# A gated cross-attention and expert network on one core: other queue and row orders in the first and last stage, and in the third two of four heads of P turned by VectorE and transfers

## The reference

```python
x = x + tanh(g_xattn[0]) * L0_xattn(layernorm(x), ctx)   # 16 heads, latent keys with rope, no mask
x = x + tanh(g_ffn[0])   * L0_ffn(layernorm(x))          # top 2 of 8 experts, low-rank terms, gelu
x = x + tanh(g_xattn[1]) * L1_xattn(layernorm(x), ctx)   # 16 heads of 32, causal softmax
x = x + tanh(g_ffn[1])   * L1_ffn(layernorm(x))          # relu, softmax over 8, V then U

# L1_xattn
qp = q @ Wq.T;  k, v = split(latent_kv @ Wkv_expand.T)
scores = einsum('bhqd,bhkd->bhqk', qh, kh) / sqrt(32);  scores = where(causal, scores, min)
out = einsum('bhqk,bhkd->bhqd', softmax(scores), vh) @ Wout.T
```

## Time and profile before

| | us |
|---|---|
| median of 3 runs | 1366.28 (1364.13 to 1367.78) |
| the profiled execution's own time | 1366.01 |
| its span | 1364.2 |
| DVE busy | 937.1 |
| ACT busy | 519.0 |
| POOL busy | 408.3 |
| first stage, about | 0 to 415 |
| second stage, about | 415 to 1010 |
| third stage, about | 1010 to 1212 |
| fourth stage, about | 1212 to 1364 |

### The profile page before, as it was taken

How to read it: one execution, slowest core, us unless ns; L and a number is a source line. 1 busy time by engine, 2 the same in 40 slices (tenths; PEclk the granted TensorE clock), 3 DMA queues, 4 the chain that set the end, 5 groups by cost and what they waited for, 6 DMA issues and landing times.

```text
span 1364.2 us, 20490 instructions
## 1 busy us (share of the span) xinstructions
PE 1338.5 (98%) x7532; PEld 1083.8 (79%) x7532; DVE 937.1 (69%) x1803; ACT 519.0 (38%) x1569; POOL 408.3 (30%) x463
## 2 busy tenths in 40 slices
PE   7999999999999999999999999999999999999999
PEld 5788888888878788778887888788876788878777
DVE  5666676675775878785778667866888777746533
ACT  2545445455554321231123111311137777712220
POOL 3113313232255343101111111114418865530000
PEclk9999999999999999999999999999999999999999
DMA  8655444443563232210221012112333131144431
GB/s 273 211 164 172 153 157 149 151 157 125 179 208 97 80 94 71 81 39 16 67 89 43 20 43 90 31 58 66 116 110 121 46 103 63 56 142 147 136 124 54
DMA packets 120136, 146.73 MB, mean 108 GB/s; under 512 B 14157, under 2 KB 75725, under 8 KB 120037
## 3 DMA queue, kind: packets, MB, share of 16 engines
q1 hardware_dynamic: 120036, 145.44, 33.5%
HBM read 101.35 MB, written 44.04 MB: 107 GB/s over the span
## 4 chain that ended last, share of the span: by engine, by line
PE 84%; DVE 9%; DMA 2%; SPq 1%; issue 1%; POOL 1%; ACT 1%; DVEq 0%; ACTq 0%; POOLq 0%
PE bank L118 80%; PE bank L121 3%; SPq L170 1%; DVE AH L130 1%; DVE STG L130 1%; DVE st L152 1%; DVE XR L140 1%; DVE PYZ L164 1%; DMA XR<-scr 1%; DVE sm L143 1%; DMA PYZ<-pscr 1%; DVE PT L130 0%; DVE XR L137 0%; DVE AH L127 0%; ACT STG L124 0%
## 5 line engine op out<-in xcount | busy, mean ns | idle before, releaser
L118 PE MATMUL bank<-XT,AR 128*128 128x512 f32 x1152 | 280.2, 393 | 0.1
L118 PE MATMUL bank<-AR 128*128 128x512 f32 x1056 | 260.5, 396 | 1.1 <-DVE PTV L127 0.7
L118 PEld LDWEIGHTS bank<-XT,AR 128*128 128x128 f32 x1152 | 213.9, 188 | 48.5 <-issue 1.5
L124 ACT ACTIVATE STG<-bank,b1c 128x512 f32<-128x512 f32 x128 | 88.3, 690 | 387.2 <-PE bank L118 319.2
L118 PEld LDWEIGHTS bank<-AR 128*128 128x128 f32 x1056 | 193.7, 188 | 46.1 <-DVE AR L130 1.5
L118 PE MATMUL bank<-AR,CT 128*128 128x512 f32 x768 | 191.3, 392 | 0.0
L118 PE MATMUL bank<-AR,AH 128*128 128x512 f32 x768 | 185.8, 390 | 0.0
L127 DVE CAST AH<-STG 128x512 fp32r<-128x512 f32 x192 | 91.3, 475 | 112.8 <-PE bank L118 98.8
L118 PEld LDWEIGHTS bank<-AR,AH 128*128 128x128 f32 x768 | 143.6, 188 | 30.7 <-issue 1.1
L118 PEld LDWEIGHTS bank<-AR,CT 128*128 128x128 f32 x768 | 140.1, 188 | 27.0 <-issue 0.4
L127 POOL CAST BA<-STG 128x256 fp32r<-128x256 f32 x64 | 31.2, 488 | 395.9 <-PE bank L118 251.8
(11 more groups left out here) (142 smaller groups left out, 1858.1 us busy)
## 6 DMA issues: line engine op xcount, KB each, us to landing
XR<-scr SPq DMA_DIRECT2D x64, 256.0 KB, 2.9
pscr<-PYZ SPq DMA_DIRECT2D x30, 512.0 KB, 2.7
PYZ<-pscr SPq DMA_DIRECT2D x120, 128.0 KB, 3.0
XR<-in_x_dram SPq DMA_DIRECT2D x32, 256.0 KB, 4.1
XR<-lscr SPq DMA_DIRECT2D x128, 64.0 KB, 2.0
scr<-XR SPq DMA_DIRECT2D x32, 256.0 KB, 2.1
STG<-in_WoT_dram SPq DMA_DIRECT2D x8, 512.0 KB, 5.3
STG<-in_Wq_dram SPq DMA_DIRECT2D x8, 512.0 KB, 5.9
```

The source lines that it names most:

```text
L118: return self.e.matmul(o, w, x, start=start, stop=stop, skip_group_check=True) if self.e else Nothing()
L124: return self.e.activation(o, x, func, **kw) if self.e else Nothing()
```

## The change

Third stage: heads 0 and 1 of P are no longer transposed by PE. DVE transposes their 32 x 32 blocks into `P3Y` (columns 2048 to 3071 of `STG`, which were slots 4 and 5 of the weights; four slots are left), SP stores them to `pscr` and loads them back in four transfers into the first half of `PTV`. AV reads them from there in four runs of 32. AV of u moves from the end of step u+2 to behind Q of step u+3. K stands ahead of the output blocks and transposes on PE, and ahead of the final additions on DVE. ACT does exponential 3 ahead of the copies of P, and all its mask seeds ahead of them. The norms of tiles (2,1,0) and (2,1,1) go from POOL to DVE. SP issues the store and the loads of P at the head of each step.

First stage: rows are loaded ahead of the first weights, two tiles are transposed ahead of `prep_a(0)`, DVE's norms stand ahead of its splits; a tile load and `prep_b(4)` go ahead of the loop on SP, later weight loads and `ln_store` go ahead of `p_store`; on DVE norm and block transpose go ahead of `pv1(u - 3, (1,))` and `blocks1`. Fourth stage: `ln_load(3, 2, .)` stands between V transfers of tile 0, `ln_load(3, 3, .)` ahead of those of tile 1.

```diff
+        P3Y, P3Z = STG[:, 2048:3072], PTV[:, 0:1024].rearrange("p (j n c) -> p n j c", j=4, n=8)
@@ tensor: opening
-            ln_turn(0, 0, 0, ring4.next())
+            for tb in range(2):
+                ln_turn(0, 0, tb, ring4.next())
             prep_a(0)
-            for tb in range(1, 4):
+            for tb in range(2, 4):
                 ln_turn(0, 0, tb, ring4.next())
@@ tensor: turn3, av3
-                for b in range(4):
+                for b in (2, 3):
                     k = ps.take(("pt3", u, b), ring.next())
...
+                pe.wait_ge(*d_p3[u, 3])
...
+                        o = k[32 * j:32 * j + 32, 128 * b:128 * b + 128]
+                        if j < 2:
+                            ins = pe.matmul(o.rearrange("p (a c) -> p a c", a=4), V3[:, b, 32 * h:32 * h + 32],
+                                            P3Z[:, 4 * j + b], True, True)
@@ tensor: step of the third stage
                     q3(u, ring3)
+                if u >= 3:
+                    av3(u - 3, ring3)
                 if u > 4 and g == 2:
                     v3(m)
+                if 0 < u < 16:
+                    k3(u, ring3)
+                if u == 1:
+                    v3(0)
                 for block in wo_at(u):
                     wo3(*block)
                 if u >= 2:
                     turn3(u - 2, ring3)
-                if 0 < u < 16:
-                    k3(u, ring3)
-                if u == 1:
-                    v3(0)
...
-                if u >= 2:
-                    av3(u - 2, ring3)
+            av3(15, ring3)
@@ scalar: step of the third stage
                     exp3(u - 1, (0, 1))
+                if u >= 3:
+                    av3(u - 3)
                 if values:
                     v3(m, 1)
                 if 1 <= u <= 16:
-                    exp3(u - 1, (2, 3) if project else (2,))
-                if seeded(u):
-                    for j in range(len(by_vector(u)), 3):
-                        seed3(u, j)
+                    exp3(u - 1, (2,))
                 if values:
                     v3(m, 3)
-                if values:
+                if 1 <= u <= 16:
                     exp3(u - 1, (3,))
+                if seeded(u):
+                    for j in range(len(by_vector(u)), 4):
+                        seed3(u, j)
                 if u >= 2:
                     turn3(u - 2, 2)
                     turn3(u - 2, 3)
@@ vector
-            ln_turn(0, 0, 0)
-            prep_a(0)
             ln_pre(0, 0, 3)
             ln_norm(0, 0, 2)
+            ln_turn(0, 0, 0)
             ln_norm(0, 0, 3)
-            for tb in range(1, 4):
-                ln_turn(0, 0, tb)
+            ln_turn(0, 0, 1)
+            prep_a(0)
+            ln_turn(0, 0, 2)
+            ln_turn(0, 0, 3)
...
+            def turn_p3(u):
+                for j in range(2):
+                    e.wait_ge(*nm3_ok[u, j])
+                    if u:
+                        e.wait_ge(*t_p3[u - 1])
+                    e.turn(blocks_out(P3Y)[:, 4 * j:4 * j + 4],
+                           blocks_in(P3[:, u % 2, 0:1024])[:, 4 * j:4 * j + 4]).then_inc(*p3y_ok.mark((u, j)))
...
                     q3_out(u)
+                if u >= 2:
+                    turn_p3(u - 2)
+                if u == 2:
+                    ln_norm(2, 1, 0)
+                    ln_norm(2, 1, 1)
...
-                if u >= 3:
-                    av3(u - 3)
                 if 1 <= u <= 16:
                     inverse(u - 1, 0)
                     inverse(u - 1, 1)
...
+                if u >= 3:
+                    av3(u - 3)
                 if u > 4 and g == 2:
                     v3(m)
+                if 1 < u < 16:
+                    k3(u)
                 for block in wo_at(u):
                     final3(*block)
-                if u >= 2:
-                    turn3(u - 2, 0)
-                    turn3(u - 2, 1)
@@ sync: opening and first stage
-            ln_load(0, 0, 1)
+            for tb in range(1, 4):
+                ln_load(0, 0, tb)
             prep_a(0)
-            ln_load(0, 0, 2)
-            ln_load(0, 0, 3)
...
             prep_a(4)
+            ln_load(*after1(0), 0)
+            prep_b(4)
...
+                if u == 2:
+                    prep_a(5)
+                    prep_b(5)
+                if u == 3:
+                    prep_a(6)
+                if u < NU and 3 <= p <= 6:
+                    ln_store(*after1(m), p - 3)
                 if 1 <= u < 31:
                     p_store(u - 1)
-                if u == 1:
-                    prep_b(4)
-                    prep_a(5)
-                if u == 2:
-                    prep_b(5)
-                    prep_a(6)
@@ sync: third stage
+            def p3_store(u):
+                e.wait_ge(*p3y_ok[u, 1])
+                if u >= 2:
+                    e.wait_ge(*d_p3[u - 2, 3])
+                e.dma(pscr[u % 2], P3Y).then_inc(*t_p3.mark(u))
+
+            def p3_load(u):
+                e.wait_ge(*t_p3[u])
+                if u:
+                    e.wait_ge(*ps.full(("av", u - 1)))
+                src = pscr[u % 2].rearrange("(j r) (i x) -> i r j x", j=4, i=4)
+                for k in range(4):
+                    e.dma(PTV[32 * k:32 * k + 32, 0:1024].rearrange("r (j x) -> r j x", j=4), src[k]).then_inc(*d_p3.mark((u, k)))
...
+                if u >= 2:
+                    p3_store(u - 2)
+                    p3_load(u - 2)
                 for tile in (ln3_tiles(u) if u < 16 else ()):
                     ln_load(*tile)
@@ sync: fourth stage
-                if m and more:
-                    for tb in range(4):
-                        ln_load(3, m + 1, tb)
...
+                    if m == 1:
+                        for tb in range(4):
+                            ln_load(3, 3, tb)
                     for tb in range(4):
                         v_store(m, tb)
+                        if m == 0 and tb:
+                            for k in ((0,), (1,), (2, 3))[tb - 1]:
+                                ln_load(3, 2, k)
```

More of the change, by code:

```diff
@@ L363, in build @@
         vy_ok, vz_ok, py_ok, pz_ok, ly_ok, lz_ok = kinds(on_dve, "vy_ok vz_ok py_ok pz_ok ly_ok lz_ok")
+        (p3y_ok,) = kinds(on_dve, "p3y_ok")
         c_mh, c_sel, rs_ok, kvc_rd, kvr_ok, kvl_ok = kinds(on_pool, "c_mh c_sel rs_ok kvc_rd kvr_ok kvl_ok")
@@ L412, in build, with normed_by_pool @@
                 xr_take("ln", 3, m, tb)
-        normed_by_pool = ((2, 1), (2, 2), (2, 3), (3, 0))
+        def normed_by_pool(ph, m, tb):
+            return (ph, m) in ((2, 1), (2, 2), (2, 3), (3, 0)) and (ph, m, tb) not in ((2, 1, 0), (2, 1, 1))
         def xr_ap(*key):
@@ L569, in ln_turn @@
                 pe.wait_ge(*ps.free(key))
-                pe.wait_ge(*(xp_ok if (ph, m) in normed_by_pool else xn_ok)[ph, m, tb])
+                pe.wait_ge(*(xp_ok if normed_by_pool(ph, m, tb) else xn_ok)[ph, m, tb])
                 for c in range(4):
@@ L991, in av3 @@
                         h = 4 * g + j
[L992 to L993 removed]
+                        o = k[32 * j:32 * j + 32, 128 * b:128 * b + 128]
+                        if j < 2:
+                            ins = pe.matmul(o.rearrange("p (a c) -> p a c", a=4), V3[:, b, 32 * h:32 * h + 32],
+                                            P3Z[:, 4 * j + b], True, True)
+                        else:
+                            ins = pe.matmul(o, V3[:, b, 32 * h:32 * h + 32],
+                                            PT3[:, 512 * j + 128 * b:512 * j + 128 * b + 128], True, True)
                 ins.then_inc(*ps.fill(("av", u)))
@@ L1394, in exp3 @@
                     if u >= 2:
-                        ac.wait_ge(*ps.full(("pt3", u - 2, j)))
+                        ac.wait_ge(*(p3y_ok[u - 2, j] if j < 2 else ps.full(("pt3", u - 2, j))))
                     for b in range(4):
@@ L1434, in scalar @@
                 m, g = divmod(u, 4)
-                project, values = bool(wo_at(u)), u > 4 and g == 2
+                values = u > 4 and g == 2
                 if 1 <= u <= 16:
                     exp3(u - 1, (0, 1))
+                if u >= 3:
+                    av3(u - 3)
                 if values:
@@ L1451, in scalar @@
                     turn3(u - 2, 3)
[L1452 to L1455, removed]
                 if u >= 16:
@@ L1903, in inverse @@
                 e.recip(S[:, 4:8], S[:, 4:8]).then_inc(*rc_ok.mark(("3", u, j)))
-            def turn3(u, b):
-                e.wait_ge(*ps.full(("pt3", u, b)))
-                if u:
-                    e.wait_ge(*ps.full(("av", u - 1)))
-                e.copy(PT3[:, 512 * b:512 * b + 512], ps.ap(("pt3", u, b))[:, :]).then_inc(*ps.drain(("pt3", u, b), on_dve))
+            def turn_p3(u):
[5 more added lines that the diff above has]
+                           blocks_in(P3[:, u % 2, 0:1024])[:, 4 * j:4 * j + 4]).then_inc(*p3y_ok.mark((u, j)))
             def av3(u):
@@ L2211, in w4_split @@
                 kind, c, hi, lo, _ = w4[n]
```

(12 more changed lines are left out.)

19 lines of the change are left out of this document (9 added, 10 removed).

## The result

The changed kernel takes 1349.58 us (median of 4 runs, 1348.33 to 1349.88) against 1365.2 us for the kernel before in the same session: ratio 0.988, 95% interval 0.9863 to 0.9896. Run again beside later experiments it took 1347.49 us, ratio 0.9861 [0.9835, 0.9887]. The forecast was 1350.2 us. The sum was right and its terms were not: the first stage's were too small and the third's too large.

What follows compares the result with a forecast made beforehand. It took PE, busy 98% of the span, as the bound, with the third stage's ACT chain 0.1 to 1 us behind. Gains 11.3 + 1.2 + 1.5 + 2.1 = 16.1 us gave 1349.9 (1350.2 against the median); 8-in-10 range 1342 to 1361.

Steps and rivals of the forecast that it cites:

- Third stage, 11.3 us: Third stage: 11.3 us gained step by step, of a ceiling of 18.8, with 15.2 us of transposes taken off PE.
- Steps 16 and 17 are full of PE work: 0.95 each: End of the third stage: PE has work throughout both steps, so each gains 0.95 us.
- Step 8: PE 12.2, all else earlier: 0.95: Third stage, step 8: PE's 12.2 us of work sets the step, everything else is earlier; gain 0.95 us.
- Opening, 1.2 us: First stage's start: PE's waits of 0.99 and 0.80 us for norms of tiles 2 and 3 shrink; 1.2 us gained.
- First trip, 1.5 us: First stage: the 1.81 us wait at 57.50 for P's first store and loads shrinks; 1.5 us gained, bounds 0 and 1.81.
- norm ahead of PV, costed at 0: First stage, DVE: norm and block transpose move 1.3 us of work past the second PV, used a step later; 0 us.
- Fourth stage, 2.1 us: Fourth stage: tiles (3,3,*) load ahead of the V stores, ending PE's 2.08 us wait at 1291.20; 2.1 us gained.
- T: Third stage: P's store and four loads, from the end of the second block transpose, take 7.3 us.
- rival (c): Third stage: the four-run read halves AV's rate, 8 us gained, 1358.2 us; chance 0.04.
- (a): Whole kernel: PE governs everywhere, ACT and DVE fold into the gaps; 24.5 us gained, 1341.8 us; chance 0.13.
- (b): Third stage: DVE and ACT take the front, only some steps gain, 5.7 us there; 10.5 in all, 1355.8; chance 0.18.
- (d): Third stage: a long T makes it slower, period (11.3 + T)/2; no gain from T = 12, 1378 at 14; chance 0.05.

Runs made afterwards that it cites:

- the kernel with the order only: The changed kernel with all four heads of P turned by TensorE again, no store or loads of P, rest of the third stage's new order kept: 1352.37 us, ratio 0.9893.

## Why the prediction was right, and where not

- **Third stage, 11.3 us:** mis-sized (its parts add up to 11.2); 5.8 in the profile, 7.3 without the half-clock stretch. The list of what is late next held in most of its parts: step 2 gained 2.5 (2.9 said; 1.9 in the profile with the stretch), step 7 0.7 (0.7), steps 10, 11, 14, 15 1.2, 0.7, 1.2, 0.6 (0.9, 0.7, 0.9, 0.6). ScalarE idled 0.38 us ahead of the AV copy in step 9 (0.5) and ended its exponentials at S+8.5 (8.6). Steps 4, 9 and 13 gained 0.4, 0.5 and 0.5 where 0 was said. Step 6 gained 0.2 (0.6): at its AV TensorE waits 0.90 us, 1.45 in the second profile, which the forecast expected only in steps 4 and 5; the two labels disagree on what ended it.
- **The step that failed first:** "Steps 16 and 17 are full of PE work: 0.95 each". AV a step later puts three AVs there instead of two (+1.1), and step 16 has no Q, so AV comes at S+1.1 while the trip lasts to S+3.4: 2.2 us. Instead of 1.9 gained, 1.1 lost: 3.0 of the miss. The rule for it was in the text ("AV waits only where a step is shorter than 9.6 us", AV "at its S+4.0"), but I applied it only to step length.
- **The second:** "Step 8: PE 12.2, all else earlier: 0.95", and step 12. Q there reads a tile whose copy stands last in ScalarE's row; 0.1 gained and 0.3 lost: 2.1 of the miss.
- **Opening, 1.2 us:** about 3. I had put it inside the two waits' 1.8; TensorE also came to full clock sooner, 6.9 to 8.9 us after its first transpose and not 10.8 to 13.1.
- **First trip, 1.5 us:** the wait went from 1.81 to 0.49. With step 6 SyncE's order is worth 2.0 to 2.7 us. The norm ahead of PV, costed at 0, was worth 3.3 us: the largest term that I did not have.
- **Fourth stage, 2.1 us:** 2.44, the waits of 2.08 and 0.23 us gone; and one chance of a half-clock stretch fewer.
- **Trip, four-run read, transposes:** T 7.1 (7.3). AV takes 1.08 us a step with heads 0 and 1 in four runs, as in the earlier trace rows: rival (c) is out. The reading by the Trainium skill, "SBUF — State Buffer", section "Specifications (TRN2)", that runs of full 16-byte lines pay nothing agrees with these 1.08 us. P's transposes fell from 272 to 144.
- **Rivals:** (a) is out: TensorE is not fully busy in ten of the fifteen windows. (b) comes out in the sum and not in the steps: its 5.7 us for the third stage are the 5.8 measured, but it had steps 6, 7, 10, 11 and 14 gain nothing, and they gain 0.2 to 1.2, and it had steps 8, 12, 16 and 17 gain 3.8, and they lose 1.3. Its cause, that ScalarE and VectorE take the front once TensorE has less to do, is right for part of the stage: 15.2 us of transposes bought 5.6. (d) is real, and steeper than I said: with a trip of 13.1 us steps 4 to 15 are 31 us longer, where my rule gave about 21, and the whole is 43 us longer. The rule had no half clock in it. Its 150 us for T = 12.5 also counted some 7 us for the seeds, where seven seeded steps, two of them with three seeds, give 5.3: 148.
- **Readings:** VectorE is at 7.2 to 10.9 us a step, not 7.4. The sum took the clock for full throughout, and the profile before had 3.41 us at half.

So 1349.9 and the profile's 1349.4 agree by luck: 5.5 us too much in the third stage met 5.7 us too little in what lies ahead of it (8.4 against 2.7). The upper bounds of the first stage's two terms (1.8 us each) did not hold.

## What to carry to other kernels

When an operation is moved a step later, write down for every step, the last ones above all, what stands directly ahead of it in its queue: that is its cover, and steps that lack it pay the whole latency. When a cheap piece of work moves past another on an engine that is not the bound, price what is queued behind both, in both directions. A wait of some 2 us on TensorE can be worth up to 1.8 us beyond its length, and a single profile cannot say how much, since half clock may or may not have come with it. Where a profile names what ended a wait, check it against what the instruction waits for in the kernel's text.

## What the runs showed of the hardware

- The granted clock fell to 0.5 (1.2 GHz) for 3.41 us at some single waits of 1.3 to 3.3 us and not at others of the same length in the same place. Each such stretch cost 0.7 to 1.8 us.
- At the start TensorE's products ran at half their later rate, 3.62 us for four that took 1.88 later. Full clock came after 10.8 to 13.1 us of the old opening and after 6.9 to 8.9 of the new one.
- A small VectorE operation on SBUF took as long as GpSimd's product beside it. In the changed kernel (first), and in the same kernel run again, where it fell on an operation that nobody waited for:

```profile
433.89 1.26 POOL L130 TENSOR_TENSOR AR<-STG,AR 128x512 fp32r<-128x512 f32 x1
433.95 1.25 DVE L130 TENSOR_TENSOR MM<-MM,sc 128x32 f32<-128x32 f32 x1
...
435.59 0.61 PE L121 MATMUL bank<-ident,MM 128*24 128x128 f32 x4 [1.84 <-DVE MM L130]
```

```profile
432.68 0.41 DVE L130 TENSOR_TENSOR MM<-MM,sc 128x32 f32<-128x32 f32 x1
...
433.12 1.33 POOL L130 TENSOR_TENSOR AR<-STG,AR 128x512 fp32r<-128x512 f32 x1
433.23 1.25 DVE L130 TENSOR_TENSOR w12c<-m 128x4 f32<-128x4 f32 x1
```

The same operation takes 0.41 or 1.25 us, by which engine came first, and TensorE's wait is 1.84 or 0.42. This was most of the 1.6 us given back ahead of the third stage. Of all 14 profiles two have this long wait, this one and that of the kernel with the order only (1.9 us); the others have 0.4 to 0.5. The Trainium skill, "SBUF — State Buffer", section "Who interferes with whom", says that a VectorE instruction with two operands from SBUF and a GpSimd instruction that reads SBUF exclude each other, and that the one that comes second waits until the first is done; both cases agree: VectorE's operation, begun 0.06 and 0.11 us after GpSimd's, ended 0.05 and 0.03 us after it.
